# A rebuilt opening of the FFN block in a one-core LayerNorm, attention and gated-FFN kernel

## The reference, cut to what matters

```python
xn = layernorm(x)                        # x: (4, 512, 1024) float32
s = attention(xn, Wq, Wk, Wv, Wo)        # 16 heads of 64, rotary, causal
xf = xn.reshape(-1, 1024)                # 2048 tokens
routing = softmax(xf @ gate_w.T)         # 8 experts, gate_w: (8, 1024)
in_scale = routing @ in_channel_scale    # (2048, 1024)
out_scale = routing @ out_channel_scale
wb = sign(weight)                        # (1024, 1024)
g = silu(((xf * in_scale) @ wb.T) * out_scale + bias)
return x + s * g
```

## Time and profile before

| | |
|---|---|
| median of three runs | 1187.37 us |
| lowest, highest | 1185.27, 1188.71 us |
| the profiled execution's own time | 1189.66 us |
| its span, first to last instruction | 1187.4 us |
| TensorE matmul busy | 1142.3 us (96%) |
| VectorE, ScalarE, GpSimd busy | 729.4, 616.2, 432.1 us |
| mean granted TensorE clock | 0.984 of full speed |

### The profile page before, as it was taken

How to read it: one execution, slowest core, us unless ns; L and a number is a source line. 1 busy time by engine, 2 the same in 40 slices (tenths; PEclk the granted TensorE clock), 3 DMA queues, 4 the chain that set the end, 5 groups by cost and what they waited for, 6 DMA issues and landing times.

```text
span 1187.4 us, 17857 instructions
## 1 busy us (share of the span) xinstructions
PE 1142.3 (96%) x5736; PEld 954.0 (80%) x5736; DVE 729.4 (61%) x1735; ACT 616.2 (52%) x1291; POOL 432.1 (36%) x258
## 2 busy tenths in 40 slices
PE   4699999999999999999999999999999998999998
PEld 3477777788888888888888888888888886888886
DVE  7676553357776777767767777767767777323133
ACT  5445344155666556656566466655665666322111
POOL 2526427433433424235333343342523523332220
PEclk9799999999999999999999999999999998999999
DMA  6734232302202022021460220202202025555652
GB/s 205 283 107 189 77 107 76 120 0 73 62 9 62 9 71 62 9 62 36 176 212 9 69 59 13 62 9 71 62 9 62 26 72 186 164 182 179 209 196 104
DMA packets 86983, 111.23 MB, mean 94 GB/s; under 512 B 3304, under 2 KB 68840, under 8 KB 85936
## 3 DMA queue, kind: packets, MB, share of 16 engines
q1 hardware_dynamic: 86960, 110.93, 28.7%
HBM read 77.37 MB, written 33.55 MB: 93 GB/s over the span
## 4 chain that ended last, share of the span: by engine, by line
PE 87%; DVE 6%; ACT 3%; POOL 2%; issue 1%; DMA 1%; SPq 0%; DVEq 0%; ACTq 0%; POOLq 0%
PE at_proj L44 17%; PE at_proj L46 17%; PE at_proj L45 17%; PE at_out L909 7%; PE at_pt L896 6%; PE ff_z_ps L264 6%; PE at_score L878 3%; PE at_score L879 3%; PE at_score L44 2%; PE at_score L45 2%; PE at_score L46 2%; PE at_proj L863 1%; POOL ff_xs_lo L601 1%; DMA w_stage<-in_L_ffn_weight_dram 1%; ACT xn_hi L365 1%
## 5 line engine op out<-in xcount | busy, mean ns | idle before, releaser
L44 PE MATMUL at_proj<-xn_hi,w_hi 128*128 128x512 f32 x896 | 363.4, 406 | 2.9 <-ACT at_v_t L1014 2.9
L46 PE MATMUL at_proj<-xn_hi,w_lo 128*128 128x512 f32 x896 | 352.0, 393 | 0.0
L45 PE MATMUL at_proj<-xn_lo,w_hi 128*128 128x512 f32 x896 | 350.8, 392 | 0.0
L46 PEld LDWEIGHTS at_proj<-xn_hi,w_lo 128*128 128x128 f32 x896 | 169.0, 189 | 37.6
L44 PEld LDWEIGHTS at_proj<-xn_hi,w_hi 128*128 128x128 f32 x896 | 169.5, 189 | 33.3 <-issue 3.3
L45 PEld LDWEIGHTS at_proj<-xn_lo,w_hi 128*128 128x128 f32 x896 | 169.8, 190 | 30.4
L1273 POOL TENSOR_TENSOR at_turning<-at_turning,rope_table 128x512 f32<-128x512 f32 x64 | 82.9, 1296 | 305.1 <-DVE at_turning L1144 305.1
L1281 POOL TENSOR_TENSOR w_lo<-w_stage,w_hi 128x1024 fp32r<-128x1024 f32 x45 | 114.5, 2559 | 162.8 <-ACT w_hi L993 162.8
L1031 ACT ACTIVATE at_prob<-at_score,at_neg_max 128x512 f32<-128x512 f32 (+3 forms) x256 | 133.4, 526 | 68.0 <-DVE at_neg_max L1172 67.6
L1040 ACT ACTIVATE at_pt_hi<-at_pt 128x512 fp32r<-128x512 f32 (+1 forms) x192 | 94.0, 524 | 101.1 <-PE at_pt L896 100.4
L1189 DVE TENSOR_TENSOR at_pt_lo<-at_pt,at_pt_hi 128x512 fp32r<-128x512 f32 (+1 forms) x192 | 111.8, 597 | 43.7 <-ACT at_pt_hi L1040 42.8
(11 more groups left out here) (129 smaller groups left out, 1827.7 us busy)
## 6 DMA issues: line engine op xcount, KB each, us to landing
z_store<-z SPq DMA_DIRECT2D x16, 512.0 KB, 2.7
w_stage<-in_L_attn_Wq_dram SPq DMA_DIRECT2D x16, 512.0 KB, 3.8
w_stage<-in_L_attn_Wk_dram SPq DMA_DIRECT2D x16, 512.0 KB, 5.1
w_stage<-in_L_attn_Wv_dram SPq DMA_DIRECT2D x16, 512.0 KB, 6.1
att_store<-at_att_t SPq DMA_DIRECT2D x32, 256.0 KB, 2.0
rope_table<-att_store SPq DMA_DIRECT2D x16, 512.0 KB, 6.5
z<-_attn_hidden_states_dram SPq DMA_DIRECT2D x16, 512.0 KB, 4.5
at_turning<-z_store SPq DMA_DIRECT2D x16, 512.0 KB, 6.1
```

The source lines that it names most:

```text
L44: pe.matmul(out, sh, mh, start=first, stop=False)
L45: pe.matmul(out, sh, ml, start=False, stop=False)
L46: return pe.matmul(out, sl, mh, start=False, stop=final)
```

## The change

- The host lays out four inputs: the weight transposed (`weight_t`), the gate weight channel-major (`gate_t`), and each channel table repeated in four zero-padded bands of 32 partitions. So the transposes of the weight and of the gate weight go, with the sign copies, the bfloat16 identity and the memset of the table staging.
- All eight blocks of weight rows have a buffer of their own (`weight_rows`, in the space of batch 1's `xn`), and are loaded without a wait; a table is one DMA. `sign(t)` writes `sign_t` directly.
- `gate(r)` is token-major for all rounds: for each tile, 16 matmuls with 128 tokens of `xn` as the stationary operand and the 16 columns of the gate table moving, 64 in a round. `gate_copy`, `gate_transposes` and their copy go.
- In the opening `chan_low` moves from GpSimd to VectorE (one operation on 64 partitions a table), and the low parts of odd k of batch 0 too (`xs_low(0, (1,))` and so on); LN(4) moves from ahead of `router(0)` to behind the last `scale` of batch 0.
- 18 idle matmuls (`warm`, into `osc_ps`) stand in the opening: 6 between the transposes of tiles 1 and 2, 4 and 8 around the second half of `gate(0)`.
- Round 0 has an order of its own: `ffn(0)` and `ffn(1)` run whole before any transpose of batch 1, and those, with `gate(1)`, stand among the matmuls of `ffn(2)`.

```diff
@@ SyncE
             load(0)
             load(1)
-            load_rows(0)
+            sp.dma_start(gate_raw[:].rearrange("p k e -> p (k e)"), io["gate_t"]).then_inc(gate_in, 16)
             load(2)
             load(3)
+            load_rows(0)
+            load_table(0)
             load_rows(1)
...
             load_rows(2)
-            load_rows(3)
+            load_table(1)
+            for t in range(3, KT):
+                load_rows(t)
             load(4)
             load(5)
-            for t in range(4, KT):
-                load_rows(t)
@@ TensorE
+            def gate(r, ts=range(QT)):
+                hi, lo = xn[r % 2]
+                for t in ts:
+                    tok = slice(t * P, (t + 1) * P)
+                    out = small_ps[:, 2 * EXPERTS * t:2 * EXPERTS * (t + 1)]
+                    pe.wait_ge(x_lo, 2 * (QT * r + t + 1))
...
+                    for k in range(KT):
+                        pe.matmul(out, hi[:, k, tok], keep["gate_t"][:, k, :], start=(k == 0), stop=False)
+                        last = pe.matmul(out, lo[:, k, tok], keep["gate_t"][:, k, :], start=False, stop=(k == KT - 1))
...
+            pe.wait_ge(ident_copies, 1)
+            warm(WARM[0])
             x_transposes(0)
-            sign_transposes(1)
             x_transposes(1)
-            gate_w_transposes()
+            warm(WARM[1])
             x_transposes(2)
             x_transposes(3)
-            sign_transposes(2)
             pe.wait_ge(tables, 1)
-            gate(0)
...
+            gate(0, (0, 1))
+            warm(WARM[2])
+            gate(0, (2, 3))
+            warm(WARM[3])
             route_transposes(0)
+            pe.wait_ge(chan_lo, 1)
+            for k in range(4):
+                in_scale(0, k)
+            pe.wait_ge(chan_lo, 2)
+            for k in range(KT):
+                ffn(0, (k,))
+                if k + 4 < KT:
+                    in_scale(0, k + 4)
+            ffn(1, range(KT))
...
+                if j == 0:
                     x_transposes(m)
+                    ffn(2, range(1))
                     x_transposes(m + 1)
+                    ffn(2, range(1, 4))
                     x_transposes(m + 2)
+                    ffn(2, range(4, 6))
                     x_transposes(m + 3)
+                    ffn(2, range(6, KT))
+                    gate(1)
+                    ffn(3, range(2))
+                    ffn(3, range(2, 4))
@@ ScalarE
+            gate_w_high()
+            ln_root(0, 2)
+            x_high(0)
+            ln_root(1, 2)
+            x_high(1)
+            chan_high(0)
             sign(0)
             x_high(2)
             x_high(3)
+            sign(1)
+            parts_copy(0)
+            sign(2)
+            route_exp(0)
             chan_high(1)
+            route_copy(0)
+            xs_high(0, range(1))
             sign(3)
+            xs_high(0, range(1, 2))
+            out_scale(0, 0)
+            xs_high(0, range(2, 4))
             sign(4)
+            xs_high(0, range(4, 5))
             sign(5)
+            xs_high(0, range(5, 6))
             sign(6)
+            xs_high(0, range(6, 7))
             sign(7)
+            xs_high(0, range(7, KT))
+            out_scale(0, 1)
+            ln_root(2, 2)
+            out_scale(1, 0)
+            out_scale(1, 1)
@@ VectorE
             layer_norm(0)
+            gate_w_low()
             layer_norm(2)
             x_low(0)
             x_low(1)
-            sign_copy(1)
-            gate_w_low()
             x_low(2)
+            chan_low(0)
             x_low(3)
-            layer_norm(4)
-            sign_copy(3)
             router(0)
             scale(0, range(2))
-            sign_copy(5)
-            sign_copy(7)
-            scale(0, range(2, 4))
+            chan_low(1)
+            xs_low(0, (1,))
+            for k in range(2, KT, 2):
+                scale(0, (k, k + 1))
+                xs_low(0, (k + 1,))
+            layer_norm(4)
+            z_scale(0)
...
+                if j == 0:
+                    x_low(m)
+                    z_scale(1)
+                    layer_norm(m + 2)
+                    x_low(m + 1)
+                    x_low(m + 2)
+                    x_low(m + 3)
+                    z_scale(2)
+                    layer_norm(m + 4)
+                    router(1)
+                    scale(1, range(4))
+                    z_scale(3)
+                    continue
```

More of the change, by code:

```diff
@@ L46, in split_matmuls, with round_of @@
     return pe.matmul(out, sl, mh, start=False, stop=final)
+ROUNDS = tuple((j, 0, QT) for j in range(BATCH))
+def round_of(tile):
+    return tile // QT
 def ffn_block(nc, block, io, keep, xn, xn_store, z_store):
@@ L187, in _ @@
         def _(pe):
[L188 to L200, removed]
             def x_transposes(n):
@@ L214, in x_transposes @@
                     last.then_inc(x_tr, 1)
[L216 to L235, removed]
+            def gate(r, ts=range(QT)):
[4 more added lines that the diff above has]
+                    pe.wait_ge(x_lo, 2 * (QT * r + t + 1))
+                    if r >= 1 and t == 0:
+                        pe.wait_ge(route_sb, r)
+                    for k in range(KT):
+                        pe.matmul(out, hi[:, k, tok], keep["gate_t"][:, k, :], start=(k == 0), stop=False)
+                        last = pe.matmul(out, lo[:, k, tok], keep["gate_t"][:, k, :], start=False, stop=(k == KT - 1))
+                if ts[-1] == QT - 1:
+                    last.then_inc(gate_mm, 1)
@@ L236, in route_transposes, with warm @@
+            def warm(count):
+                for _ in range(count):
+                    pe.matmul(osc_ps[:], keep["ident_r"][:], keep["ident_r"][:].unsqueeze(1).to_broadcast([P, QT, P]),
+                              start=True, stop=True)
+            def route_transposes(r):
+                pe.wait_ge(route_ok, 2 * (r + 1))
+                for t in range(ROUNDS[r][2] - ROUNDS[r][1]):
                     last = pe.transpose(small_ps[:, t * P:(t + 1) * P].bitcast(F32R), route4[:, t, :], keep["ident_r"][:])
@@ L429, in _ @@
                 m = n + QT
+                if j == 0:
+                    x_high(m)
+                    out_scale(2, 0)
+                    x_high(m + 1)
+                    ln_root(3, 2)
+                    out_scale(2, 1)
+                    x_high(m + 2)
+                    x_high(m + 3)
+                    ln_root(4, 2)
+                    out_scale(3, 0)
+                    parts_copy(1)
+                    route_exp(1)
+                    out_scale(3, 1)
+                    route_copy(1)
+                    xs_high(1, range(4))
+                    continue
                 out_scale(n, 0)
@@ new lines, in xs_low, with chan_low @@
+            def xs_low(r, ks):
+                for k in ks:
+                    dve.wait_ge(xs_h, KT * r + k + 1)
+                    dve.tensor_tensor(xs_lo[:, k, :], xs_full[:, k % 2, :], raw(xs_hi[:, k, :]), ALU.subtract)\
+                       .then_inc(xs_l[k % 2], 1)
+            def chan_low(c):
+                table = keep[("chan_in", "chan_out")[c]]
+                dve.wait_ge(chan_hi, c + 1)
+                dve.tensor_tensor(table[64:P, :], chan_rows[64:P, c, :], raw(table[64:P, :]), ALU.subtract).then_inc(chan_lo, 1)
@@ L1364, in build @@
             keep["rope_in"], keep["z_add"], keep["xn_ok"] = sem("rope_in"), sem("z_add"), sem("xn_ok")
-            xn = [[sb(with_xn, f"xn{b}_{part}", [P, KT, SEQ], F32R) for part in ("hi", "lo")] for b in range(2)]
+            xn = [[sb(with_xn, f"xn0_{part}", [P, KT, SEQ], F32R) for part in ("hi", "lo")]]
+            with ExitStack() as opening:
+                keep["weight_rows"] = sb(opening, "weight_rows", [P, KT, EMBED], F32)
+            xn.append([sb(with_xn, f"xn1_{part}", [P, KT, SEQ], F32R) for part in ("hi", "lo")])
             with ExitStack() as with_ffn:
```

381 lines of the change are left out of this document (185 added, 196 removed).

## The result

The kernel after takes 1218.59 us (median of 4 runs, 1217.55 to 1220.14), the kernel before 1186.36 beside it (4 runs, 1185.27 to 1188.71): ratio 1.027, 95% interval 1.0248 to 1.0292. The change costs 32 us. The forecast was 1187.0, the range 1180.5 to 1192.5: wrong, and on the side that had the smallest chance (0.22). The two profiled executions differ by less, 1187.4 and 1215.8 us, 28.4, since the one before was slower than its four timed runs (1189.66) and the one after the fastest of its four (1217.55).

A forecast was written before the change was run, and what follows sets the result against it. TensorE, holding 87% of the chain, was taken as the bound. Round 0 and the opening gave -1.7 us, later gates +1.4: -0.3 from the median 1187.37, so 1187.0 us, range 1180.5 to 1192.5.

The forecast's parts named there:

- Step 2: Router and token-major gate: 0.075 us a matmul, 4.8 us a round; in the opening `scale` comes 11.2 us earlier.
- weight loads bound the gate: Rival on the gates: 0.117 us a matmul, 9.3 us more in all, 1196.3 us; chance 0.16.
- Step 1: Opening, to the last `x_low` of batch 0: the weight wait goes, and it ends at 22.1 against 25.9.
- Steps 2 and 3: Router of the opening, then `ffn(0)`: it starts at 35.7, 13.4 us earlier, and ends at 47.4; 12.4 us gained.
- one of the two low parts waits: Before `ffn(0)`: VectorE's `chan_low(1)` meets GpSimd's `xs_low(0)`; one waits 0.95 us, or nothing if they overlap.
- Idle matmuls cost nothing: Opening: the 8 last end before routes come; the 4 take 0.9 to 1.7 where TensorE would wait for `x_lo`.
- Step 4: From VectorE's late LN(4) to `in_scale(1,0)` at 88.5 against 90.18: of 12.4 us gained 1.7 is left.
- the gap at tile 6: TensorE stands from 64.35 to 68.75, 4.4 us, before tile 6's transposes; half clock behind it adds 1.3 us.
- the gap at `osc_ps`: In the middle of `ffn(1)` TensorE waits 2.8 us for `out_scale(1,0)`; the clock is taken as staying up.
- that rival, +2.5 us: Rival: the clock falls after the 2.8 us gap at `osc_ps` too, +2.5 us, 1189.5 us; chance 0.2.
- Step 5: Later rounds: gates 2 and 3 count in full, 2 x (4.8 - 4.07) = +1.4 us; attention is unchanged.

The follow-up runs named there:

- e3: The changed kernel with 128 instead of 16 columns moving in each of the 64 gate matmuls, same weight loads: 1198.02 us, ratio 1.0088.
- e4: The changed kernel with one unused buffer of 32 bytes a partition ahead of the router's buffers: 1218.02 us, ratio 1.026.
- e5: e1 with every FFN buffer at the offset it has in the kernel before: 1189.36 us, ratio 1.0026 to the kernel before.
- e6: e5 with LN(4) ahead of `router(0)` and the loads of tiles 4 and 5 earlier: 1186.88 us, ratio 1.0003 to the kernel before.
- e7: e6 with the order of round 0 of the kernel before: 1179.38 us, ratio 0.9932 to the kernel before.
- e9: e7 with LN(4) and the loads of its tiles back behind the last `scale` of batch 0: 1184.62 us, ratio 0.9984.
- e8: The changed kernel with the gates of rounds 1 to 3 spread, four gate matmuls behind each of 16 `ffn` matmuls: 1223.3 us, ratio 1.0295.
- e1: The changed kernel with the old gate (16 matmuls of 512 moving columns, copy, transposes) in all rounds: 1189.91 us, ratio 1.0017.

## Why the prediction was wrong

**Step 2, the gate: the term that failed.** I took 0.075 us a matmul, 4.8 us a round, between the row of transposes and the row of fp32r loads. It is 0.111 at full clock: the upper bound, the distance of the four fp32r loads, was the truth, and the transposes were not the same case: their stationary operand has 128 columns too, but 16 partitions and float32, against 128 and fp32r; which of the two makes the difference wasn't tried. By the rule of the Trainium skill (TensorE: Matmul & The Clock Gate, "LDWEIGHTS") 128 columns are estimated at 107 ns; 0.111 at full clock agrees. The rival "weight loads bound the gate" had this mechanism and gave 1196.3 us; e3, where only this is true, measured 1198.0. So this term alone would have left the range of 1180.5 to 1192.5.

**What no rival had: the clock.** I asked whether gaps would lower it, and never whether a dense run of small matmuls would. I took it as full inside every gate. In all four gates it went to 1.2 GHz, 1.2 us after the first one's start and 2.8 to 3.8 after the others', while TensorE had no idle time; e3 shows that 128 columns a matmul at the same distance keep it. The Trainium skill (TensorE: Matmul & The Clock Gate, "Part 1: The HAM clock gate (the "warmup" mystery)") puts the lower clock down to idle time and the higher one to sustained matmuls. The windows of 84.37 to 98.40 contradict that reading, with busy shares of 100% at 0.51. The price is 20.6 of the 28.7 us. With the distance at 0.213 a gate takes 10 to 11 us: over twice the 4.8 of my sum, and beyond its upper bound of 7.5.

**Step 1 was right.** VectorE resumed at 13.39 (13.15 forecast), the last `x_low` ended at 22.4 (22.1).

**Steps 2 and 3, the rest.** The gate of the opening ended at 33.21, not 25.5. From there the walk holds: the Exp stands behind `sign(2)` and the table load as forecast (33.51, 34.58), routes are ready at 37.4, 4.2 after the gate (4.1 forecast), and `ffn(0)` starts at 42.96, 9.75 behind the gate (10.2 forecast). (42.96, like my 35.7, is the first matmul into `ff_z_ps`; its row before is 49.56, so the 49.13 that I subtracted from was one matmul early, 13.4 for 13.9. The sum doesn't use it.) That one of the two low parts waits was right: beside VectorE's `chan_low` GpSimd's took 2.14 instead of 1.29 us at 40.76, 0.85 more (0.95 forecast), and then VectorE's own 1.37 instead of 0.69 at 42.08. "Idle matmuls cost nothing" was half wrong: in after the 4 at 24.67 stand on the path for 1.85 us, since at half clock the first half of the gate outlasts `x_low`.

**Step 4 was right in nearly every number.** From the first matmul of `ffn(0)` to the end of the gap at tile 6 I had 33.05 us, measured 33.30; the gap at `osc_ps` 2.8, measured 2.25; the one at tile 6 4.4, measured 4.05, with the clock at half behind it. The clock stayed up behind the first gap, as taken; in e3, e4 and e5 it did not, so on that rival, +2.5 us, my reason (the gap is the shorter) was no reason, and the hit was luck. `in_scale(1,0)` at 102.23 instead of 88.5 is 7.3 us of late start, 5.3 of `gate(1)`, which I had as hidden behind VectorE, and 1.1 of the rest, the half clock behind the gate included.

**Step 5** had +0.7 us a gate in rounds 2 and 3; it was +9.57 and +7.87 with the half clock behind it and the pairs.

**Left out altogether:** the placement of the buffers, 0.012 us a pair. And the reading that the new order of round 0 was given: I took its gaps as the price of the earlier start. e6, e7 and e9 show that 8.3 of the 9.9 us by which `ffn(0)` starts earlier in e7 (39.64) can be kept, if LN(4) is done while TensorE and ScalarE do the router and if VectorE's work on batch 1 begins during `ffn(0)`.

Not settled: which buffer sets the pair distance, when a mixture of large and small matmuls loses the clock, and behind which gaps of 2 to 3 us it falls.

## What to carry to other kernels

Few moving columns behind a full weight load save nothing on TensorE and, many in a row, can halve its clock, for the work behind them too: price such a run by the load distance, look at the granted clock inside it, and prefer the orientation that streams many columns. An opening that ends earlier gives its gain back wherever another engine's work was moved behind it; follow that engine through the next round before counting the gain. After a rebuild, measure the distance of matmuls that were not touched: it may have moved with the buffers.

## What the runs showed of the hardware

- The granted clock fell to 1.2 GHz on a TensorE that was 100% busy with matmuls of 16 moving columns 0.111 us apart, and stayed at 2.4 GHz with 128 columns at the same distance (e3, all four gates). With four such matmuls behind each of 512 columns it fell as well (e8).
- Streaming 128 instead of 16 columns behind a 128-column fp32r weight load cost no time: 0.11 us both ways.
- Moving SBUF buffers, with nothing else changed, moved the distance of the `ffn` matmuls: 0.468 us a pair in e1 and 0.457 in e5, which has the offsets of the kernel before (0.456); 32 bytes more ahead of the router's buffers (e4) made 0.465 of 0.468.
- Behind one and the same gap at `osc_ps` the clock stayed up after 2.25 us (after) and 2.26 (e1), and fell at once after 2.25 (e3), 2.28 (e4) and 2.37 (e5). Behind the gap in attention's first part it stayed up after 2.86 to 2.88 us (e1, e5, e6) and fell after 2.87 to 2.89 (after, before, e7).
- In the first transposes of an execution the profile's clock reads 1.00 (9.00 to 20.00), yet eight take 1.92 us, as at 0.50 (1.94 at 76.26 in after) and not as later (1.10 at 15.25): look at the distances as well as at the clock.
- Two-operand elementwise work on VectorE and GpSimd at one time: the one that began first kept its time, the other waited. GpSimd took 2.14 instead of 1.29 us behind a VectorE operation begun 0.2 earlier (40.55, 1.22 us), VectorE then 1.37 instead of 0.69.
